# Second attention with head chunks outside and samples inside, its output paths and half of the next FFN's preparation among the later slots

## The reference

```
x = x + attn_a(layernorm(x))        # 16 heads of 8, weights from a distance
x = x + ffn(layernorm(x))
x = x + attn_b(layernorm(x))        # 16 heads of 8, rotary positions, softmax
x = x + ffn(layernorm(x))           # the same weights again

attn_b: q, k, v = split(x @ qkv_w.T + qkv_b); q, k = rope(q), rope(k)
        out = softmax(q k^T / sqrt(8)) v per head      # [16 heads, 8 samples, 256 tokens, 8]
        return out.reshape(8, 256, 128) @ proj_w.T + proj_b     # head is the outermost axis
ffn:    scores = sigmoid(x @ router_w.T); groups of 8 experts, the best 4 of 8 groups,
        the best 8 of 64 experts, weights normalised, times 2.5 -> coef [T, 64]
        sum over 64 experts of ((silu(x Wg) * (x Wu)) * coef) Wd  +  one shared expert
```

## Time and profile before

| | us |
|---|---|
| median of 3 runs | 1136.32 |
| lowest and highest | 1131.87, 1139.19 |
| the profiled execution: span from first to last instruction | 1128.1 |
| its own time, span and what lies around it | not given apart from the span; the median lies 8.2 above the span |
| busy: TensorE, VectorE, ScalarE, GpSimd | 974.6, 982.1, 695.7, 354.8 |
| mean granted TensorE clock, as a share of full speed | 0.859 |

### The profile page before, as it was taken

The page is one execution under the profiler, slowest core; times in us unless marked ns, Lnnn a source line. Parts: engine busy times, 40 slices in busy tenths (PEclk is TensorE's granted clock), DMA queues, the critical chain, the costliest instruction groups (busy, mean ns, idle before and its releaser), DMA issues. The chain is left out here.

```text
span 1128.1 us, 17423 instructions
## 1 busy us (share of the span) xinstructions
PE 974.6 (86%) x5403; PEld 708.3 (63%) x5403; DVE 982.1 (87%) x1491; ACT 695.7 (62%) x794; POOL 354.8 (31%) x214
## 2 busy tenths in 40 slices
PE   7746676766768999999999899999759999999997
PEld 5523343434446888888888645444647888888886
DVE  7798889888978999999999797996598999999997
ACT  4759999999975455544444562667444544444554
POOL 2036555655550334333332120100012333333430
PEclk9865555555558999999999998999969999999999
DMA  2000000000104855555551000000028655555531
GB/s 57 1 1 1 1 0 1 1 1 1 36 15 97 217 153 147 153 148 158 151 155 40 1 1 1 1 2 1 1 71 196 168 149 157 151 156 153 150 90 37
DMA packets 36478, 85.16 MB, mean 75 GB/s; under 512 B 5968, under 2 KB 19280, under 8 KB 36432
## 3 DMA queue, kind: packets, MB, share of 16 engines
q1 hardware_dynamic: 36432, 84.56, 28.2%
HBM read 82.45 MB, written 2.10 MB: 75 GB/s over the span
## 5 line engine op out<-in xcount | busy, mean ns | idle before, releaser
L1324 ACT ACTIVATE sg<-ps 128x512 f32<-128x512 f32 x264 | 156.8, 594 | 265.6 <-PE ps L473 264.1
L473 PE MATMUL ps<-xh,whi 128*128 128x512 f32 x528 | 206.6, 391 | 1.3 <-ACT b L1189 1.3
L473 PE MATMUL ps<-xh,wlo 128*128 128x512 f32 x528 | 206.3, 391 | 0.0
L473 PE MATMUL ps<-xl,whi 128*128 128x512 f32 x528 | 206.2, 391 | 0.0
L2070 DVE TENSOR_TENSOR hf<-sg,ps 128x512 f32<-128x512 f32 x264 | 170.3, 684 | 32.0 <-DVE hl L2077 24.4
L1471 POOL TENSOR_TENSOR rr<-xr,rr 128x2048 f32<-128x2048 f32 x32 | 144.9, 4548 | 163.5 <-ACT xr L1170 149.4
L1518 POOL CAST whi<-wraw 128x384 fp32r<-128x384 f32 x66 | 66.4, 1006 | 369.7 <-PE ps L473 321.5
L2077 DVE TENSOR_TENSOR hl<-hf,hh 128x1024 fp32r<-128x1024 f32 x132 | 179.1, 1357 | 0.5 <-DVE hf L2070 0.5
L2082 DVE TENSOR_TENSOR hf<-hf,cbc 128x1024 f32<-128x1024 f32 x128 | 157.5, 1231 | 13.3
L1372 ACT ACTIVATE hh<-hf 128x1024 fp32r<-128x1024 f32 x132 | 139.2, 1054 | 4.8 <-DVE hf L2082 4.8
L1520 POOL TENSOR_TENSOR wlo<-wraw,whi 128x384 fp32r<-128x384 f32 x66 | 117.4, 1778 | 5.3
(11 more groups left out here) (259 smaller groups left out, 1581.1 us busy)
## 6 DMA issues: line engine op xcount, KB each, us to landing
cbc<-routing_coefficients SPq DMA_DIRECT2D x256, 256.0 KB, 3.8
wraw<-in_wexp_dram SPq DMA_DIRECT2D x66, 192.0 KB, 2.8
X<-in_x_dram SPq DMA_DIRECT2D x4, 256.0 KB, 4.9
routing_coefficients<-cT SPq DMA_DIRECT2D x8, 128.0 KB, 2.3
out_dram<-X SPq DMA_DIRECT2D x4, 256.0 KB, 2.9
rope_in<-in_consts_dram SPq DMA_DIRECT2D x1, 512.0 KB, 3.5
wa<-in_wA_dram SPq DMA_DIRECT2D x1, 256.0 KB, 4.2
w_in<-in_wB_dram SPq DMA_DIRECT2D x1, 128.0 KB, 3.3
```

What stands on the lines that cost most here:

```text
L473: return pe.matmul(o, l, r, start=start, stop=stop, **kw)
L1324: act.activation(sg[c % 2][:, :], bank(4 + 2 * (c % 2)), ACT.Silu).then_inc(s_sg, 1)
```

## The change

**Order of units.** A new `unit_b(U)` makes the head chunk the outer loop and the samples the inner one: sixteen slots are one chunk, in two halves of four samples. So the first chunk is complete for all samples after 16 of 64 units, and `o_all` now has whole chunks early. `shift` and `copy_out` take 512 tokens of one chunk instead of two chunks of 256.

**Output path among the slots.** TensorE's `b_path_step`, VectorE's slot loop and ScalarE's carry the path for chunk 0 in slots 36 to 46 and for chunk 1 in slots 52 to 62, all in bank 7, between the steps of the maxima. Token-major is no longer a transposition but an fp32 multiplication with 36 of the identity's columns (nine for each of four heads), so that a half fits one bank. Chunk 2 and the first half of the FFN's preparation (normalising, transposing, logits, sigmoid) follow in the tail (`b_tail_step`), chunk 3 and the second half in `last_of_b`. `route_bests`, `route_groups` and `route_masks` of the first half stand among chunk 3's steps on VectorE; `route_experts` of the first half and routing of the second stay in `prepare_f(1)`, the second half's `lows` now last.

**Norm.** The reciprocal standard deviation is exp(-0.5 ln(var + eps)) on ScalarE (`f_norm_rstd`), whose functions are in the table set of the slots' exponentials; groups 0 to 2 are normalised by GpSimd, group 3 by ScalarE.

**Meetings.** GpSimd and SyncE don't wait for the fourth meeting: SyncE loads the first weights when all shifted q are there, and GpSimd prepares them between its normalised groups 1 and 2; a new semaphore `s_last` takes the place of the fifth meeting. Routing tiles get addresses of their own behind a pad.

The diff, cut to what the steps touch:

```diff
+        def unit_b(U):
+            G = U // UNITS
+            return 4 * (G % 2) + U % UNITS // 2, G // 2, 2 * (U % 2)
 # SyncE
-            meet(sp, 4)
+            sp.sem_inc(s_phase, 1)
+            sp.wait_ge(s_q2, 2 * B)
             load_first(1)
             load_second(1)
-            sp.sem_inc(s_phase, 1)
+            sp.sem_inc(s_last, 1)
+            sp.wait_ge(s_s2, B * UNITS)
+            sp.wait_ge(s_oTs, B + CHUNKS)
             first_coefs(1)
 # TensorE
+                if s == 4:
+                    pe.wait_ge(s_on, B + 2)
+                elif s == 5:
+                    pe.wait_ge(s_ores, B + 1)
...
+            def token_major(c, half, n):
+                wanted = ident.rearrange("p (j x) -> p j x", x=32)[:, :, 0:VH]
+                for r in range(8):
+                    last = mm(bank(n)[:, r * 4 * VH:(r + 1) * 4 * VH].rearrange("p (j x) -> p j x", x=VH),
+                              o_all[:, c, :].rearrange("p (l r) -> p r l", r=16)[:, 8 * half + r, :], wanted)
+                last.then_inc(s_oP, 1)
+            def b_path_step(V):
+                if V in (36, 52):
+                    c = (V - 36) // 16
+                    pe.wait_ge(s_bev, 4 * (c + 1))
+                    pe.wait_ge(s_q2, 2 * (V // UNITS))
+                    token_major(c, 0, 7)
+                elif V in (38, 54):
+                    c = (V - 38) // 16
+                    pe.wait_ge(s_on, B + 2 * c + 1)
+                    token_major(c, 1, 7)
+                elif V in (43, 59):
+                    c = (V - 43) // 16
+                    pe.wait_ge(s_q2, 2 * (V // UNITS))
                     pe.wait_ge(s_on, B + 2 * c + 2)
+                    transposed(c, 7)
+                elif V in (45, 61):
+                    projected((V - 45) // 16, 7)
+            def b_tail_step(U):
+                if U == 53:
+                    pe.wait_ge(s_mx, 2 * B * UNITS - 1)
+                    f_transposed(1, 0, 0)
+                elif U == 55:
+                    pe.wait_ge(s_mx, 2 * B * UNITS)
+                    logits(1, 0, 0)
+                elif U == 56:
+                    f_transposed(1, 0, 1)
+                elif U == 57:
+                    pe.wait_ge(s_q2, 2 * B)
+                    pe.wait_ge(s_bev, 3 * CHUNKS)
+                    token_major(2, 0, 7)
+                elif U == 58:
+                    logits(1, 0, 1)
+                    token_major(2, 1, 0)
+                elif U == 60:
+                    pe.wait_ge(s_on, B + 6)
+                    transposed(2, 7)
+                elif U == 61:
+                    projected(2, 0)
+            def last_of_b():
                 pe.wait_ge(s_bev, 2 * B)
+                token_major(3, 0, 2)
+                token_major(3, 1, 3)
+                pe.wait_ge(s_on, B + 8)
+                transposed(3, 4)
+                projected(3, 5)
+                f_transposed(1, 1, 0)
+                pe.wait_ge(s_ores, B + 3)
+                logits(1, 1, 0)
+                f_transposed(1, 1, 1)
+                logits(1, 1, 1)
 # ScalarE
+                act.preload_act_table_set("natural_log_exp_and_others")
                 for U in range(B * UNITS + 3):
...
+                    if U in (32, 48):
+                        o_transposed_b((U - 32) // 16, 7)
+                    elif U == 42:
+                        f_norm_rstd(0)
+                    elif U == 53:
+                        f_norm_rstd(1)
+                    elif U == 59:
+                        scores(1, 0)
+                        act.preload_act_table_set("natural_log_exp_and_others")
+                    elif U == 60:
+                        o_transposed_b(2, 7)
+                    elif U == B * UNITS:
+                        f_norm_rstd(2)
+            def f_norm_rstd(g):
+                act.wait_ge(s_fstat, GROUPS + g + 1)
+                st.do(act.activation(std[g][:, :], mv[g][:, :, 1], ACT.Ln, bias=eps_s[:, 0:1]))
+                st.sync()
+                act.activation(rstd[g][:, :], std[g][:, :], ACT.Exp, scale=-0.5).then_inc(s_fstd, 1)
+            def last_of_b():
+                act.wait_ge(s_fxT, GROUPS + 2)
+                f_high(0)
+                f_high(1)
+                o_transposed_b(3, 4)
+                act.wait_ge(s_fxnT, GROUPS + 3)
+                act.activation(f_xT[2][:, :], bank(7), ACT.Copy).then_inc(s_fxT, 1)
+                f_norm_rstd(3)
+                act.wait_ge(s_fxT, GROUPS + 3)
+                f_high(2)
+                f_norm_apply_group(1, 3)
+                act.preload_act_table_set("sigmoid_and_others")
+                act.wait_ge(s_fxnT, 2 * GROUPS)
+                act.activation(f_xT[3][:, :], bank(6), ACT.Copy).then_inc(s_fxT, 1)
+                scores(1, 1)
...
 # GpSimd
+                for g in range(3):
+                    f_norm_apply_b(g)
+                    if g == 1:
+                        pool.wait_ge(s_q2, 2 * B)
+                        prepare_experts(1)
+            def f_norm_apply_b(g):
+                pool.wait_ge(s_foff, GROUPS + g + 1)
+                for j in range(GTILES):
+                    last = pool.tensor_scalar(f_xn[g][:, j, :], X[:, g * GTILES + j, :], rstd[g][:, j:j + 1],
+                                              f_off[g][:, j:j + 1], ALU.mult, ALU.add)
+                last.then_inc(s_fxn, 1)
 # VectorE
+                    if V in (37, 53):
+                        normalise((V - 37) // 16, 0, 7)
+                    elif V in (39, 55):
+                        normalise((V - 39) // 16, 1, 7)
+                    elif V in (46, 62):
...
+                        residual((V - 46) // 16, 7)
+                    elif V == 51:
                         stats_of(0)
+                    elif V == 56:
+                        offset(0)
+                max_rows(B - 1)
+                stats_of(1)
+                copy_xT(0, 0)
+                shift(B - 1, 0)
+                offset(1)
+                shift(B - 1, 1)
+                copy_xT(1, 0)
+                normalise(2, 0, 7)
+                normalise(2, 1, 0)
+                marks()
+                residual(2, 0)
                 stats_of(2)
+                route_bests(1, 0)
+                route_groups(1, 0)
+                offset(2)
+                normalise(3, 0, 2)
+                normalise(3, 1, 3)
+                route_masks(1, 0)
+                residual(3, 5)
                 stats_of(3)
+                lows(1, 0)
+                offset(3)
```

More of the change, by code:

```diff
@@ L44 @@
 ROUTE_SCALE = 2.5
+ROUTE_PAD = 7424
 C_ID, C_HS, C_ROT, C_COS, C_SIN, C_END = 0, 128, 144, 272, 784, 1296
@@ L205, in hybrid @@
                     f_xT = [sr(f"f_xT{g}", [P, GT]) for g in range(GROUPS)]
[L206 to L222, removed]
+                    f_off = b_off
                 hf = [sb(f"hf{s}", [P, FF_PAIR]) for s in range(2)]
@@ L869, in pv_b @@
                     pe.wait_ge(s_bev, C // 2)
-                last = pv(vt, s, c, wr[:, C % CHUNKS, :], bank(6)[:, c % 2 * N:(c % 2 + 1) * N], (half,))
+                last = pv(vt, s, c, wr[:, C % CHUNKS, :], bank(6)[:, C % 2 * N:(C % 2 + 1) * N], (half,))
                 if half == MT - 1:
@@ L886, in samples_b @@
                         b_max_step(V)
[L888 to L901, removed]
-                    pe.wait_ge(s_on, B + 2 * c + 2)
[L903 to L912, removed]
-                pe.wait_ge(s_bev, 2 * B)
[L915 to L924, removed]
-                for g in range(2):
-                    logits(1, 0, g)
@@ new lines, in transposed, with projected @@
+            def transposed(c, n):
+                for j in range(4):
+                    last = pe.transpose(bank(n)[:, j * P:(j + 1) * P], b_otok[c % 2][:, j, :], ident)
+                last.then_inc(s_oT, 1)
+            def projected(c, n):
+                pe.wait_ge(s_oTs, B + c + 1)
+                for j in range(4):
+                    last = mm(bank(n)[:, j * P:(j + 1) * P], b_oT[c % 2][:, j * P:(j + 1) * P], wo_b[:, :])
+                last.then_inc(s_wo, 1)
+            def b_path_step(V):
[11 more added lines that the diff above has]
+                    pe.wait_ge(s_q2, 2 * (V // UNITS))
+                    pe.wait_ge(s_on, B + 2 * c + 2)
+                    transposed(c, 7)
+                elif V in (45, 61):
+                    projected((V - 45) // 16, 7)
@@ L1348, in prepare_f @@
                     f_norm_copy(f, 1)
[L1349 to L1357 removed]
+                    scores(f, 1)
                 coef_copies(f, 0)
@@ L1786, in prepare_f @@
             def prepare_f(f):
[L1788 to L1795 removed]
                 route_experts(f, 0)
[L1797 removed]
+                if f == 0:
+                    lows(f, 1)
                 route_bests(f, 1)
@@ L1801, in prepare_f @@
                 route_experts(f, 1)
+                if f == 1:
+                    lows(f, 1)
             def samples_a():
@@ L2048, in o_of_b, with offset, copy_xT @@
-                dve.wait_ge(s_foff, GROUPS + 2)
```

(10 more changed lines are left out.)

184 lines of the change are left out of this document (91 added, 93 removed).

## The result

| | before | after |
|---|---|---|
| median, us | 1134.09 | 1166.16 |
| profiled execution: span, us | 1128.1 | 1161.2 |
| mean granted TensorE clock | 0.859 | 0.826 |

The ratio of after to before, measured side by side, is 1.0273, 95% interval 1.0245 to 1.03: slower, where no change was forecast, and above the forecast's range (1124 to 1144). One of after's four executions ran in a slower state (1589.11 us); it is in the median of the table and not in the ratio, and the median of the other three is 1162.95, which is also the time of the profiled one.

The account below looks back on a forecast made before the run. TensorE and VectorE nearly full in the slots, then a serial chain of 54.5 us. Its gain of 23.3 is spent in slots (12.1) and tail (11.4): 1136.3 + 0.1 = 1136.4 us, range 1124 to 1144.

Parts of the forecast that it names:

- the token-major price: TensorE, each token-major half: 16 instructions at 0.111, 1.78 us, between bounds of 1.05 and 1.90.
- the clock: TensorE's clock, 1.00 until 818, then mean 0.68; an earlier or later drop moves logits and transpositions some 1.2 us.
- slots 12.1: Slots 36 to 63: added steps make the last maximum 12.1 us later, bounds 7.1 and 16.2.
- tail 27.2: From last maximum to last copy-out: grows from 15.8 to 27.2 us through ScalarE's queue; lower bound 21.7.
- behind it 31.2: From last copy-out to the FFN's third gate chunk: serial output path, norm and routing shrink from 54.5 to 31.2 us.
- The 8.2 us: Runs' median 1136.32 beyond the page's span of 1128.1; the same 8.2 us taken for the changed kernel.
- (1): Slots and tail: the additions hide, later maximum only 7.1, tail 21.7; 10.5 us less, 1126; chance 0.20.
- (2): Slots and tail don't grow at all, the whole 23.3 us is gained: 1113; chance 0.07.
- (3) Lockstep: Slots: TensorE and VectorE stop each other through two score banks, growth 16.2 instead of 12.1: 1140.5; chance 0.15.
- (4) Draining at table switches: Slot 59 in the tail: a second 1.28 behind each of two table loads, 2.6 us more: 1139.0; chance 0.05.
- ScalarE's gap ahead of the first rstd: Tail: ScalarE, through with exponential 53 at 0.85, waits for group 1's statistics until 2.75 us after the last maximum.
- TensorE waits 0.38 us ahead of the third projection, 2 to 3 were forecast: Tail: TensorE waits 2 to 3 us for ScalarE's copy ahead of the third projection.

Follow-up runs that it names:

- The contiguous run: The changed kernel with ScalarE writing the attention's result so that token-major's 36-column multiplications read weights side by side: 1159.26 us, ratio 1.0233.
- the form alone, in the old place: The kernel before with only its token-major transpositions replaced by 36-column fp32 multiplications, behind the slots: 1158.37 us, ratio 1.0237.
- the 128-column form: The changed kernel with token-major in quarters, as fp32 multiplications with the whole identity instead of transpositions: 1147.69 us, ratio 1.0142.
- the version with the tail fillers: The transposed version plus nine unused 512-column multiplications in TensorE's pauses in the tail: 1125.36 us, ratio 0.9958.
- the two runs above: Token-major in quarters in the changed kernel: by 128-column multiplications (1147.69 us, ratio 1.0142) and by transpositions (1129.09 us, ratio 0.9986).
- the transposed version: The changed kernel with token-major as transpositions again, four quarters a chunk, one bank each: 1129.09 us, ratio 0.9986.
- the last run: The kernel before with token-major in its old place as 36-column fp32 multiplications, token rows written side by side: 1172.81 us, ratio 1.0359.

## Why the prediction was wrong

**The step that failed** is the token-major price, "each half is 8 fp32 multiplications ... I take 1.78 (16 x 0.111)", bounded by 1.90. A half took 3.69. The bound came from logits and projection, whose weights (`f_xT`, `b_oT`) lie side by side; `o_all` is read with a stride, and there the price is 0.23 an instruction. The contiguous run, at 2.4 GHz, gives 1.98. For eight halves that is 8 x (3.69 - 1.78) = 15.3 us, about half of the 31 us by which the FFN goes on later.

**The other half is the clock,** which the prediction named for the stretch behind only ("move by some 1.2 us"); in its slots and its tail it put the clock at nothing. Behind the first token-major step it is at 1.2 GHz for most of the remaining slots and of the tail, and what stands there takes 1.7 to 1.8 times as long (eight values 1.08 for 0.64 us, a projection 2.08 for 1.16). In the slots the 36-column form brings it: the clock fell at both chunks in after and in the contiguous version and, with the form alone, in the old place; behind the 128-column form of about the same length and behind transpositions there were at most dips of 3 us (0.77 above; 0.66 from 765 to 770 in the version with the tail fillers). In the slots length is worth about 9.3 us and clock 12.9 (the two runs above). In the tail the form is not alone: there the clock falls with transpositions too. The prediction also took the clock to be at 1.00 until 818, from rows that begin at 731; before, it is at 0.50 from 677 to 687, and early in the slots of every other kernel here too, so the full clock of the earlier trace rows was not to be taken for granted:

```profile
680.00:685.00 5.00, 4.77 (x15) 3.24 (x15) 4.52 (x10) 0.00 (x0) 0.00 (x0) 0.50 0.00 0
```

**With the form taken out, the sum came near.** By transposition each half costs 0.73 less (1.78 - 1.05), so the forecast's terms become: slots 12.1 less 2.9 = 9.2, measured 6.3; tail 27.2 less 1.5 = 25.7, there 30.5, with the tail fillers and a full clock 25.8; behind it 31.2 less 1.5 = 29.7, there 29.9. Together that is 5.7 us earlier, measured 3.6; in part luck, as the slots were taken too long and the tail too short. So the mechanism, that the gain behind the tail is spent in slots and tail, is shown; with the change as it stands the price of a token-major half and that of the clock were far above the forecast.

**The total.** The 8.2 us that the sum puts on top of the span set the median of some executions against the span of another. An execution's time lies 1.7 to 1.9 above its own span in every run here, so the forecast of 1136.4 was some 6 us too high for that reason; the forecast of no change does not hang on it.

**The rivals.** (1) and (2), the additions hide: not in after; the transposed slots (6.3) lie between that version's lower bound (7.1 less 2.9 = 4.2) and its 9.2, but the tail doesn't hide. (3) Lockstep: the slots grew by 28.5, beyond the 16.2 of this rival. VectorE idles 34.3 us ahead of its maxima in after, 13.0 before, nearly all waiting for TensorE; by transposition, with more steps among the slots, it is 13.1. The groups of maxima in after, before and the transposed version (busy us, mean ns, idle before them and what ended it):

```profile
L2069 DVE TENSOR_REDUCE mx<-ps 128x2 f32<-128x512 f32 x128 | 82.5, 685 | 34.3 <-PE ps L484 32.9
L1964 DVE TENSOR_REDUCE mx<-ps 128x2 f32<-128x512 f32 x128 | 82.6, 684 | 13.0 <-PE ps L473 12.0
L2072 DVE TENSOR_REDUCE mx<-ps 128x2 f32<-128x512 f32 x128 | 82.5, 683 | 13.1 <-PE ps L484 11.8
```

TensorE was slow; steps among the slots alone did not make the two stop each other. (4) Draining at table switches did not show. ScalarE's timeline of after:

```profile
832.11 1.28 ACT L1415 ACT_TABLE_LOAD   x1
833.40 0.66 ACT L1415 ACTIVATE sc<-ps 128x256 f32<-128x256 f32 x2
834.08 1.28 ACT L1344 ACT_TABLE_LOAD   x1
835.37 1.02 ACT L1332 ACTIVATE wr<-ps 128x1024 f32<-128x1024 f32 x1
```

Each load is followed within 0.02 us, as in the earlier trace rows. The further 1.38 us that the Trainium skill (ScalarE: Activation LUTs, "What ACT_TABLE_LOAD costs") puts on a switch does not appear in this trace either.

**The smaller steps.** Right: ScalarE's gap ahead of the first rstd, GpSimd's normalised group (1.74 us for four, 1.6 taken), the loop's length. The first stands on ScalarE's timeline of after:

```profile
814.22 0.30 ACT L1356 ACTIVATE std<-mv,eps_s 128x4 f32<-128x4 f32 x1 [1.87 <-DVE mv L1681]
```

The second stands on GpSimd's:

```profile
815.53 1.74 POOL L1621 TENSOR_SCALAR f_xn<-X,rstd,b_off 128x128 f32<-128x128 f32 x4 [15.49 <-DVE b_off L2127]
```

Wrong in after: TensorE waits 0.38 us ahead of the third projection, 2 to 3 were forecast, because TensorE itself is late there; with transpositions it is 1.58, and with the tail fillers as well, at full clock, 2.10. Behind the tail 36.4 us for 31.2: token-major (7.16 for both halves, 3.6 taken) is most of it.

**What stays open.** Why the clock falls behind some steps and not behind others: the runs tell which steps it fell behind, not why; it also fell where no token-major step was near (677 before, 771 in the last run). How the tail's growth divides into length and clock is not shown. The 2.4 us by which the slots begin later in after lie ahead of the changed code in time; the contiguous version, with the same tiles, begins its slots at 670.2, so they are no fixed price of the change.

## What to carry to other kernels

A price taken from a neighbouring instruction held here only for operands of the same layout: before a price per instruction is taken from a neighbour, compare the strides of its weights as well as its shape. When short steps are put among the work of a full TensorE, read the granted clock in narrow stretches on both sides of them, since what they cost may stand in the rows of everything behind. And where TensorE has pauses in a stage, filling them can pay: nine unused multiplications went with a full clock and a tail shorter by 4.7 us here, while others, between the thin multiplications, only made the program longer.

## What the hardware showed that was not expected

An fp32 multiplication with weights 64 bytes apart took 0.23 us an instruction with 36 columns at either clock, and 0.25 with 128 columns at 2.4 GHz; with contiguous weights 36 columns took 0.12 at 2.4 GHz and 0.23 at 1.2. A transposition of the same strided data took 0.18 (0.72 for four), and 0.13 in a row of 16. The clock fell while TensorE was shown as busy in 5.00 of 5.00 us (740 to 745 in after). ScalarE's copy of 128x512 took 1.047 us when it wrote with a stride, 0.59 without.
